# Attention B of a four-stage model on one core: the softmax division is done at the residual add, and each head's output projection has its own half of a bank

## The reference, cut to what matters

```python
def _L0_attn_b_ref(x, wq, wk, wv, wo):       # x is the layernorm of the residual rows
    q, k, v = (jnp.einsum('bim,mhd->bhid', x, w) for w in (wq, wk, wv))   # 16 heads of 128
    q, k = rope(q), rope(k)
    mult = jnp.asarray(ATTN_SCALE ** 0.5, dtype=x.dtype)
    s = jnp.einsum('bhid,bhjd->bhij', q * mult, k * mult)
    s = s - jnp.asarray(INFTY_APPROX, dtype=s.dtype) * mask      # causal
    p = jax.nn.softmax(s, axis=-1)
    o = jnp.einsum('bhij,bhjd->bhid', p, v)
    r = jnp.einsum('bhid,hdm->bim', o, wo)
    return r
...
x = x + _L0_attn_b_ref(_layernorm(x, axis=-1), ...)
```

## Time and profile before

| | |
|---|---|
| median of three runs | 1718.75 us |
| the profiled execution's own time | 1719.37 us |
| its span in the profile | 1717.3 us |
| TensorE busy | 1638.6 us, 95% of the span |
| VectorE busy | 1195.2 us, 70% |
| ScalarE busy | 945.4 us, 55% |
| GpSimd busy | 619.6 us, 36% |
| mean granted TensorE clock | 0.982 of full speed |
| attention B | from about 806 us to 1431 us of the span |
| in it, `scale`'s multiplications (L1133) | 256, 139.6 us busy |
| in it, `add_out` (L1144) | 64, 43.5 us busy |

### The profile page before, as it was taken

How to read it: one execution, slowest core, us unless ns; L and a number is a source line. 1 busy time by engine, 2 the same in 40 slices (tenths; PEclk the granted TensorE clock), 3 DMA queues, 4 the chain that set the end, 5 groups by cost and what they waited for, 6 DMA issues and landing times. The chain is left out here.

```text
span 1717.3 us, 29230 instructions
## 1 busy us (share of the span) xinstructions
PE 1638.6 (95%) x9656; PEld 1370.5 (80%) x9656; DVE 1195.2 (70%) x2766; ACT 945.4 (55%) x2300; POOL 619.6 (36%) x479
## 2 busy tenths in 40 slices
PE   6799999999988999997899999999999998999998
PEld 4577777777767888886789888888888886888887
DVE  6488888888897555557576777777677688655555
ACT  3577777777754333332676676666677664233332
POOL 3555555555530000001565565565565450000000
PEclk9799999999999999999899999999999999999999
DMA  2100000000001001001000000000000001000001
GB/s 90 37 16 15 15 15 0 15 15 15 1 1 62 19 19 37 0 0 51 5 20 13 19 6 19 6 20 23 6 19 6 0 1 33 24 19 19 18 1 49
DMA packets 10634, 32.21 MB, mean 19 GB/s; under 512 B 1088, under 2 KB 5184, under 8 KB 10560
## 3 DMA queue, kind: packets, MB, share of 16 engines
q1 hardware_dynamic: 10560, 31.28, 5.5%
HBM read 29.18 MB, written 2.10 MB: 18 GB/s over the span
## 5 line engine op out<-in xcount | busy, mean ns | idle before, releaser
L378 POOL TENSOR_TENSOR ab_swapped<-ab_swapped,const 128x512 f32<-128x512 f32 x128 | 168.9, 1319 | 237.2 <-ACT ab_swapped L373 236.9
L1404 ACT ACTIVATE f_silu<-ps 128x512 f32<-128x512 f32 x128 | 76.3, 598 | 283.0 <-PE ps L116 283.0
L1514 DVE TENSOR_TENSOR f_hidden<-ps,f_silu 128x512 f32<-128x512 f32 x128 | 87.7, 690 | 202.0 <-PE ps L116 202.0
L114 PE MATMUL ps<-xh,f_wl 128*128 128x512 f32 x512 | 203.2, 397 | 1.5 <-DVE f_hidden L1514 1.5
L115 PE MATMUL ps<-xl,f_wh 128*128 128x512 f32 x512 | 202.8, 396 | 0.0
L116 PE MATMUL ps<-xh,f_wh 128*128 128x512 f32 x512 | 202.6, 396 | 0.0
L1233 POOL TENSOR_TENSOR ab_qk<-ab_qk,ab_swapped 128x512 f32<-128x512 f32 x128 | 173.9, 1359 | 10.0
L378 DVE TENSOR_TENSOR ab_qk<-ps,const 128x512 f32<-128x512 f32 x128 | 88.1, 689 | 110.5 <-PE ps L116 110.5
L701 DVE TENSOR_SCALAR aa_probs<-aa_probs,aa_inv 128x256 f32<-128x256 f32 x256 | 157.2, 656 | 4.5
L1025 ACT ACTIVATE ab_probs<-ab_probs,ab_negmax 128x128 f32<-128x128 f32 (+1 forms) x256 | 114.5, 449 | 77.3 <-DVE ab_negmax L1123 76.5
L114 PE MATMUL ps<-f_wh,f_hl 128*128 128x256 f32 x512 | 144.4, 282 | 3.3 <-DVE x L1530 3.3
(11 more groups left out here) (186 smaller groups left out, 4817.6 us busy)
## 6 DMA issues: line engine op xcount, KB each, us to landing
f_stage<-wf_in SPq DMA_DIRECT2D x16, 768.0 KB, 4.2
b_stage<-wb_qkv_in SPq DMA_DIRECT2D x8, 768.0 KB, 4.2
a_stage<-wa_in SPq DMA_DIRECT2D x8, 608.0 KB, 3.8
x<-x_in SPq DMA_DIRECT2D x4, 512.0 KB, 7.6
bo_stage<-wb_out_in SPq DMA_DIRECT2D x8, 256.0 KB, 2.5
out<-x SPq DMA_DIRECT2D x4, 512.0 KB, 2.9
const<-const_in SPq DMA_DIRECT2D x1, 704.0 KB, 5.9
open_small_in<-small_weights SPq DMA_DIRECT2D x1, 392.0 KB, 7.4
```

Source lines behind the costliest of these rows:

```text
L114: nc.tensor.matmul(out, ll, rh, start=start, stop=False)
L378: return engine.tensor_tensor(by_batch(out), by_batch(src), table(c, rows, col), ALU.mult)
L1514: nc.vector.tensor_tensor(hidden[:, m, :], UP(m), silu[:, m, :], ALU.mult).then_inc(hid_done, 1)
```

## The change

The probabilities stay unscaled: `scale` becomes `invert`, which only takes the reciprocal of the row sums and keeps it for the whole slot. `turn` waits for the exponentials rather than for the scaled probabilities. A row sum belongs to one token and one head, so the two heads' output projections are no longer accumulated onto each other: for one tile of 128 tokens, head 0 goes to the left half of the bank and head 1 to the right half, each is multiplied by its own inverse row sum and added to the residual rows. `output` now works on one token tile (6 products, index t from 0 to 3) instead of two (12 products), and its four calls stand in steps 2, 3, 3 (behind the two projections) and 0. `add_out` is two dependent operations of 128x256 for each token tile. The first waits for the products; the second waits for the first. The weight split `split_wo` and `normalise_stats` each move one step later. At the end the outputs rotate over three banks.

```diff
-        negmax, total, inv = (sb(n, [P, PAIRS, 2]) for n in ("negmax", "total", "inv"))
+        negmax, total = (sb(n, [P, PAIRS, 2]) for n in ("negmax", "total"))
+        inv = sb("inv", [P, NG, PAIRS, 2])
...
-                pe.wait_ge(scaled, g + 1)
+                pe.wait_ge(exp_done, g + 1)
...
-            def output(it, s, i, bank=OUT):
+            def output(it, s, t, bank=OUT, before=1):
...
-                for t in range(2):
-                    tok = slice((2 * i + t) * P, (2 * i + t + 1) * P)
-                    for h in range(2):
-                        ins = matmul3(nc, bank[:, t * D:(t + 1) * D], (mh[:, s % 2, h, tok], ml[:, s % 2, h, tok]), (woh[:, h, :], wol[:, h, :]), h == 0, h == 1)
+                after(pe, out_added, TG * n + t + 1 - before)
+                tok = slice(t * P, (t + 1) * P)
+                for h in range(2):
+                    ins = matmul3(nc, bank[:, h * D:(h + 1) * D], (mh[:, s % 2, h, tok], ml[:, s % 2, h, tok]), (woh[:, h, :], wol[:, h, :]), True, True)
...
-                if j >= 2 and not (first and s == 0) and not (last and s == NG - 1 and j == 3):
+                if j >= 2 and not (first and s == 0):
                     output(*moved(it, s, 0, -PAIRS)[:2], j - 2)
+                if j == 0 and not (first and s <= 1):
+                    output(*moved(it, s, 0, -2 * PAIRS)[:2], 3)
                 if j == 3 and not (last and s >= NG - 2):
                     project(*moved(it, s, 0, 2 * PAIRS)[:2], 0)
                     project(*moved(it, s, 0, 2 * PAIRS)[:2], 1)
+                if j == 3 and not (first and s == 0):
+                    output(*moved(it, s, 0, -PAIRS)[:2], 2)
...
-            output(HP - 1, NG - 2, 1)
+            output(HP - 1, NG - 2, 3, S(0), 3)
             norm_turn(nc, c, norm, pe, 1, norm_banks)
-            output(HP - 1, NG - 1, 0, S(0))
-            output(HP - 1, NG - 1, 1, S(1))
+            output(HP - 1, NG - 1, 0, S(1), 3)
+            output(HP - 1, NG - 1, 1, OUT, 3)
+            output(HP - 1, NG - 1, 2, S(0), 3)
+            output(HP - 1, NG - 1, 3, S(1), 3)
...
-                for q in range(2):
-                    ins = nc.vector.tensor_scalar(probs[:, j, span[q]], probs[:, j, span[q]], inv[:, j, q:q + 1], None, ALU.mult)
-                ins.then_inc(scaled, 1)
+            def invert(it, s, j):
+                dve.wait_ge(exp_done, pair_no(it, s, j) + 1)
+                nc.vector.reciprocal(inv[:, s, j, :], total[:, j, :]).then_inc(inv_done, 1)
...
-                nc.vector.tensor_tensor(c.x[:, t:t + 2, :], bank.rearrange("p (t d) -> p t d", d=D), c.x[:, t:t + 2, :], ALU.add).then_inc(out_added, 1)
+                for h, done in ((0, half_added), (1, out_added)):
+                    if h == 1:
+                        dve.wait_ge(half_added, u + 1)
+                    nc.vector.scalar_tensor_tensor(out=c.x[:, at, :], in0=bank[:, h * D:(h + 1) * D], scalar=inv[:, s, 2 * h + t // 2, t % 2:t % 2 + 1], in1=c.x[:, at, :], op0=ALU.mult, op1=ALU.add).then_inc(done, 1)
...
-                    scale(*moved(it, s, j, 1))
-                if j == 0 and not (first and s <= 1):
-                    add_out(*moved(it, s, 0, -2 * PAIRS)[:2], 1)
-                if j == 3 and not (first and s == 0):
-                    add_out(*moved(it, s, 0, -PAIRS)[:2], 0)
+                    invert(*moved(it, s, j, 1))
                 if not (last and s == NG - 1 and j >= 2):
                     row_max(*moved(it, s, j, 2))
+                if j >= 2 and not (first and s == 0):
+                    add_out(*moved(it, s, 0, -PAIRS)[:2], j - 2)
+                if j <= 1 and not (first and s <= 1):
+                    add_out(*moved(it, s, 0, -2 * PAIRS)[:2], j + 2)
...
-                if last and (s, j) in ((2, 1), (3, 1)):
+                if last and (s, j) in ((2, 2), (3, 2)):
                     normalise_stats(s - 2)
```

More of the change, by code:

```diff
@@ L814, in attention_b @@
         proj_ready, rope_read, rotated, values_done = sem("proj_ready"), sem("rope_read"), sem("rotated"), sem("values_done")
-        scores_ready, maxed, exp_done, inv_done, scaled = sem("scores_ready"), sem("maxed"), sem("exp_done"), sem("inv_done"), sem("scaled")
+        scores_ready, maxed, exp_done, inv_done = sem("scores_ready"), sem("maxed"), sem("exp_done"), sem("inv_done")
         turned, probsT_done, pv_done, mix_hi, mix_lo = sem("turned"), sem("probsT_done"), sem("pv_done"), sem("mix_hi"), sem("mix_lo")
-        vproj_ready, out_ready, out_added = sem("vproj_ready"), sem("out_ready"), sem("out_added")
+        vproj_ready, out_ready, half_added, out_added = sem("vproj_ready"), sem("out_ready"), sem("half_added"), sem("out_added")
         swap_done, sin_done = sem("swap_done"), sem("sin_done")
@@ L920, in mix @@
                 nc.tensor.matmul(out[:, P:T], v(1), probsT[:, j % 2, T:W], start=False, stop=True).then_inc(pv_done, 1)
-            def output(it, s, i, bank=OUT):
+            def output(it, s, t, bank=OUT, before=1):
                 n = slot_no(it, s)
-                if i == 0:
+                if t == 0:
                     pe.wait_ge(mix_lo, 2 * n + 2)
@@ L930, in output @@
                         pe.wait_ge(wo_lo, it + 1)
-                if bank is OUT:
-                    after(pe, out_added, 2 * n + i)
-                else:
+                if bank is not OUT:
                     pe.wait_ge(exp_done, PAIRS * NG * HP)
-                for t in range(2):
-                    tok = slice((2 * i + t) * P, (2 * i + t + 1) * P)
-                    for h in range(2):
-                        ins = matmul3(nc, bank[:, t * D:(t + 1) * D], (mh[:, s % 2, h, tok], ml[:, s % 2, h, tok]), (woh[:, h, :], wol[:, h, :]), h == 0, h == 1)
+                after(pe, out_added, TG * n + t + 1 - before)
+                tok = slice(t * P, (t + 1) * P)
+                for h in range(2):
+                    ins = matmul3(nc, bank[:, h * D:(h + 1) * D], (mh[:, s % 2, h, tok], ml[:, s % 2, h, tok]), (woh[:, h, :], wol[:, h, :]), True, True)
                 ins.then_inc(out_ready, 1)
@@ L1008, in split_wo @@
                 act.wait_ge(wo_in, 16 * (it + 1))
-                after(act, out_ready, 2 * NG * it)
+                after(act, out_ready, TG * NG * it)
                 nc.scalar.copy(woh[:], wo_stage[:]).then_inc(wo_hi, 1)
@@ L1045, in mixed_hi @@
                 act.wait_ge(pv_done, PAIRS * n + 2 * h + 2)
-                after(act, out_ready, 2 * (n - 1))
+                after(act, out_ready, TG * (n - 1))
                 nc.scalar.copy(mh[:, s % 2, h, :], MIX(h)).then_inc(mix_hi, 1)
@@ L1067, in step @@
                     split_hi(it + 1, j // 2)
-                if s == 0 and j == 3:
+                if s == 1 and j == 0:
                     split_wo(it)
@@ L1139, in mixed_lo, with add_out @@
                 nc.vector.tensor_tensor(ml[:, s % 2, h, :], MIX(h), mh[:, s % 2, h, :].bitcast(F32), ALU.subtract).then_inc(mix_lo, 1)
-            def add_out(it, s, i, bank=OUT):
-                dve.wait_ge(out_ready, 2 * slot_no(it, s) + i + 1)
-                t = s * TG + 2 * i
-                nc.vector.tensor_tensor(c.x[:, t:t + 2, :], bank.rearrange("p (t d) -> p t d", d=D), c.x[:, t:t + 2, :], ALU.add).then_inc(out_added, 1)
+            def add_out(it, s, t, bank=OUT):
+                u, at = TG * slot_no(it, s) + t, s * TG + t
+                dve.wait_ge(out_ready, u + 1)
+                dve.wait_ge(inv_done, PAIRS * (slot_no(it, s) + 1))
+                for h, done in ((0, half_added), (1, out_added)):
+                    if h == 1:
+                        dve.wait_ge(half_added, u + 1)
+                    nc.vector.scalar_tensor_tensor(out=c.x[:, at, :], in0=bank[:, h * D:(h + 1) * D], scalar=inv[:, s, 2 * h + t // 2, t % 2:t % 2 + 1], in1=c.x[:, at, :], op0=ALU.mult, op1=ALU.add).then_inc(done, 1)
             def step(it, s, j):
@@ L1172, in step @@
                         rope(*moved(it, s, 0, 2 * PAIRS)[:2], 1)
-                if s == 1 and j == 0:
+                if s == 1 and j == 1:
                     split_wo(it)
-                if last and (s, j) in ((2, 1), (3, 1)):
+                if last and (s, j) in ((2, 2), (3, 2)):
                     normalise_stats(s - 2)
@@ L1180, in normalise_stats @@
             def normalise_stats(s):
-                dve.wait_ge(out_added, 2 * slot_no(HP - 1, s) + 2)
+                dve.wait_ge(out_added, TG * slot_no(HP - 1, s) + TG)
                 norm_stats(nc, c, norm, dve, s)
@@ L1203, in _ @@
             row_max(0, 0, 1)
-            scale(0, 0, 0)
+            invert(0, 0, 0)
             for it in range(HP):
@@ L1207, in _ @@
             mixed_lo(HP - 1, NG - 1, 1)
-            add_out(HP - 1, NG - 2, 1)
+            add_out(HP - 1, NG - 2, 2)
+            add_out(HP - 1, NG - 2, 3, S(0))
             normalise_stats(NG - 2)
@@ L1211, in _ @@
             norm_rows(nc, c, norm, dve, NG - 2)
-            add_out(HP - 1, NG - 1, 0, S(0))
-            add_out(HP - 1, NG - 1, 1, S(1))
```

(4 more changed lines are left out.)

5 lines of the change are left out of this document (removed).

## The result

The changed kernel takes 1708.9 us (median of four runs, 1707.2 to 1709.7), the kernel before 1718.9 us beside it. The ratio is 0.9938, 95% interval 0.9926 to 0.9951: 10 us faster, against a forecast of 1709.1.

The account below looks back on a forecast made before the run. TensorE's waits were taken to bound the steady slots, VectorE's work the end. Against the profiled 1719.4 us, -17.4 + 2 + 1 - 1.2 + 6.0 = -9.6 gave 1709.8, median 1709.1 us; range for 8 in 10, 1702 to 1717.

Parts of the forecast that it names:

- The bound and where the gain lies: 29 slots of attention B: TensorE waits 17.4 us in them, the most the steady part can give; 17.89 us per stall-free slot.
- The chain behind the stall: Step 0: multiplication beside GpSimd and add delay row_max, exponentials and swap 2, so step 1's products start 0.43 us late.
- The work taken from VectorE: Whole kernel: multiplications go, -149.9 us of VectorE's busy time; with the dearer adds, 71 us less work in all.
- Last slot of a head pair, 2 us kept: Products wait there for split_lo part 1: some 0.3 of 0.95 us stay, 7 times, 2 us.
- `split_lo` part 0, +1: Third slot, step 3: the split now stands behind the add of t = 0; 0.15 us, 7 times, bounds 0 and +4.5.
- The single bank in quarters: Each output call waits for the add before it; hand count finds all in time, so nothing lost in ordinary slots.
- The price of an add, 0.91 us: VectorE's two dependent half-adds per token tile: 0.91 us, against 0.60 per two tiles before.
- The start, -1.2: Start of attention B: first transposes no longer wait for scaled probabilities; -1.2 us, bounds 0 and -2.5.
- The end, +6.0: Third slot's step 2 to the experts: VectorE has no gap after the last row_max; +6.0 us, bounds +3 and +8.5.
- A: Rival: the stalls go and the end costs little, +6 becoming 0; 1703 us, chance 0.13.
- B: Rival: the single bank makes TensorE wait anew, 0.25 us a slot, 8 us; 1717 us, chance 0.16.
- C: Rival: GpSimd holds up the new add, 0.85 us a slot, 27 us; 1736 us, chance 0.09.

Follow-up runs that it names:

- run 6: The kernel before with GpSimd's two rotation operations cut from 512 to 16 columns: 1693.4 us.
- run 3: The kernel before with row_max first and the output projection's second half moved from step 3 to step 0 of the next slot: 1705.6 us.
- run 1: The changed kernel with the multiplications of the probabilities back on VectorE, written to a spare buffer nobody reads: 1712.6 us.
- Run 10: The changed kernel with 16 identity transposes on TensorE while it waits in the last step before output t = 2: 1705.8 us.
- run 4: The changed kernel with the last mix of attention B placed before the last step's output product t = 2: 1705.1 us.

## Why the prediction was right

*The bound and where the gain lies.* Right. TensorE waited 17.4 us in the 29 slots by my count; 18.15 were gained. The slot without stalls is 17.82 us, not 17.89 (29 x 0.07 = 2 us). Step by step against the slot from 1058.56, step 3 is 0.02 us shorter and steps 0 and 2 together 0.04 to 0.05; the estimate took off the stall of step 1 alone.

*The chain behind the stall (multiplication beside GpSimd, add, row_max, exponentials, swap).* Right, step by step in the timelines, and shown by run 6. But it isn't the only way out, and the prediction did not separate the division from the order. With the division where it was, order alone gave 15.5 of the 18.15 us (run 3); with the multiplications back, unread, the slots lost only 1.9 (run 1).

*The work taken from VectorE.* Over-counted: the 149.9 us add up two groups that overlap in time, together 139.6. VectorE's busy time fell by 67.0 us in the whole (1195.2 to 1128.2), not 71. The sum does not rest on it.

*Last slot of a head pair, 2 us kept.* Mis-sized: nothing is left (17.83 us, against 18.84). I took the weight split at its 1.50 us; it took 0.89 on average, since GpSimd's operations fall elsewhere now. *`split_lo` part 0, +1.* Right: third slots take 18.07, 0.25 us each, 1.7 in all; it took 1.22 us, as estimated.

*The single bank in quarters.* Right: no call of `output` waits in the slots. *The price of an add, 0.91 us.* Right for most pairs, 0.1 us short for some: the last four take 3.81 us. The rule of a fixed cost for each instruction ("VectorE: DVE Perf Modes", the section on the TRN2 errata, in the Trainium skill) gives an estimate of 0.42 us for a half; measured is 0.48, and the measurement decides.

*The start, -1.2.* Right (-1.2), apart from the clock's two levels.

*The end, +6.0.* Right in kind, 2.1 us too small. The hand count met the chip to 0.1 us up to the last row_max (+14.5 from step 2; measured 1394.91 - 1380.39 = 14.52). The step that failed is the sentence that VectorE has no gap from there. It waited 1.76 us for the cast of the last mix, which stood behind a product that waited 1.87 us for an add and then, with the mix, ran at TensorE's lower clock. Run 10 puts 1.3 us of it on the clock; run 4 takes 1.8 away by order. The other 0.3 us are the nine adds, 8.5 us from each start to the next operation's where the count had 8.2.

The errors have opposite signs: the gain in the slots was put 3.7 us too low, the cost of the end 2.1 too low, and 1.3 came from outside attention B. With 0.3 more in the two steps between, they cancel. That the sum of -9.6 us came out to the tenth is luck; its terms were good to about 4 us.

*The rivals.* A (the end costs nothing) falls with 39.7 us; B (waits at the single bank) with slots of 17.82; C (the new add held by GpSimd) with a maximum of 486 ns in 256.

## What to carry to other kernels

Where one engine is at its limit in a steady loop, ask how late each of its hand-overs comes, not how full the others are: here VectorE could take on a third more work in the slots at almost no cost, and 15 us came by order alone. Moving one operation forward moves all behind it in that engine's list: look at every step of the loop, not only at the one with the stall. A form of the work that is free inside the loop can be dear where the loop ends, where nothing hides it: here the half-adds cost nothing in the slots and 4.4 us for eight in the end; let the last rounds use another form.

## What was not expected of the hardware

A float32 multiplication of VectorE that reads and writes SBUF took 828 ns on average beside GpSimd and 297 without it, and a subtraction of two SBUF tensors 1.50 and 0.68 us, while an operation on a bank and an SBUF tensor kept to 0.47 to 0.49 (256 columns) or 0.68 to 0.69 (512) in all 320 cases. After a wait of TensorE of 1.9 us in the end the granted clock of the five microseconds around it was 0.71; 16 idle transposes in the wait kept it at 1.00, and that was worth 1.3 us. The same stretch at the start of attention B ran at 0.64 or at 1.00 in single executions of programs that differ only 550 us later; that stays open.
